# Earlier B copies, a split shared between DVE and ACT, and three drives moved from DVE to POOL in a Mamba scan

## What is computed

```python
x_d, z = jnp.split(jnp.einsum('btm,im->bti', x, W_in), 2, axis=-1)
x_d = _silu(conv_over_4_tokens(x_d) + conv_b)
dt_raw, B_mat, C_mat = split(jnp.einsum('btd,kd->btk', x_d, W_x))      # 1 + 16 + 16 columns
delta = jax.nn.softplus(dt_raw * W_dt[:, 0] + b_dt)
def step(h, inp):
    d_t, b_t, c_t, u_t = inp
    dA = jnp.exp(d_t[..., None] * A)
    h = dA * h + d_t[..., None] * b_t[:, None, :] * u_t[..., None]
    return h, jnp.einsum('bds,bs->bd', h, c_t)
y = (ys + D_param * x_d) * _silu(z)
h = _layernorm(x + y @ W_out.T)
scores = sigmoid(h @ gate_w.T)       # the best 4 of 8 groups, then 8 experts, weights normalised
out = _layernorm(h + experts(h) + shared(h))
```

## Time and profile before

| | |
|---|---|
| median of 3 runs | 1238.26 us (1237.28 to 1240.08) |
| the profiled execution's own time | 1239.62 us |
| its span, first to last instruction | 1237.8 us |
| mean granted TensorE clock | 0.926 |
| busy: PE, DVE, ACT, POOL | 1001.2, 1012.7, 639.0, 780.3 us |
| slot 0 of tile 5 to slot 0 of tile 6 | 403.33 to 478.32 us |

### The profile page before, as it was taken

One profiled execution on the slowest core, in us unless ns is written; L12 is line 12 of the kernel. 1 busy time (PEld: TensorE's weight loads), 2 busy tenths in 40 slices (PEclk: granted clock), 3 DMA queues, 4 the chain that ended last, 5 costly groups with the idle time before them and its releaser, 6 DMA issues.

```text
span 1237.8 us, 16888 instructions
## 1 busy us (share of the span) xinstructions
PE 1001.2 (81%) x4739; PEld 764.4 (62%) x4739; DVE 1012.7 (82%) x1914; ACT 639.0 (52%) x1662; POOL 780.3 (63%) x935
## 2 busy tenths in 40 slices
PE   3898878988788987879888786765299999999960
PEld 3776656666566665666656564443178888888850
DVE  7499999999999999999999999893334477777763
ACT  1575554646446464554645546431056666666640
POOL 7234376776767677687776777667600367677675
PEclk7999999999999999999999999878599999999985
DMA  4399401111021120101101010157355688988872
GB/s 171 121 328 325 130 22 37 42 34 42 26 60 33 34 63 13 58 26 44 53 26 48 3 51 25 34 196 298 95 152 172 204 252 261 277 266 265 268 220 80
DMA packets 104475, 150.28 MB, mean 121 GB/s; under 512 B 13983, under 2 KB 91231, under 8 KB 103999
## 3 DMA queue, kind: packets, MB, share of 16 engines
q1 hardware_dynamic: 87487, 107.39, 26.8%
q0 software_dynamic: 16896, 41.80, 11.8%
HBM read 72.32 MB, written 76.82 MB: 120 GB/s over the span
## 4 chain that ended last, share of the span: by engine, by line
DVE 39%; PE 29%; issue 15%; POOL 6%; DMA 1%; ACT 0%; DVEq 0%; SPq 0%; POOLq 0%; ACTq 0%
DVE arena L1320 20%; PE BC L979 11%; PE Y L826 4%; DVE arena L1307 3%; PE Y L973 3%; PE K L991 3%; PE F L991 3%; POOL gat L688 2%; DVE arena L1332 2%; PE K L838 2%; POOL pool_dram L627 2%; PE D L985 1%; DVE arena L1288 1%; DVE arena L1283 1%; DMA mixer_own<-pool_dram 1%
## 5 line engine op out<-in xcount | busy, mean ns | idle before, releaser
L1320 DVE TENSOR_TENSOR_SCAN arena<-D,arena 128x444 f32<-128x444 f32 (+1 forms) x352 | 350.9, 1037 | 6.3 <-ACT D L1067 5.2
L826 PE MATMUL Y<-arena,ident 128*128 128x444 f32 (+1 forms) x704 | 311.0, 571 | 1.6 <-DVE arena L1332 1.6
L688 POOL DMA_INDIRECT gat<-y_dram,slot_all x176 | 174.9, 994 | 148.6 <-DMA y_dram<-mixer_own 84.8
L1067 ACT ACTIVATE D<-mixer_own,aneg 128x216 f32<-128x216 f32 (+1 forms) x384 | 150.5, 427 | 151.5 <-DVE arena L1320 148.5
L1067 ACT ACTIVATE D<-arena,aneg 128x216 f32<-128x216 f32 x320 | 128.8, 438 | 141.2 <-DVE arena L1320 141.1
L627 POOL DMA_INDIRECT pool_dram<-hrow,slot_of x176 | 169.1, 961 | 49.4 <-issue 42.6
L639 POOL TENSOR_TENSOR arena<-mixer_own,arena 128x888 f32<-128x888 f32 (+1 forms) x72 | 130.8, 1816 | 101.2 <-ACT arena L1055 99.8
L1332 DVE TENSOR_TENSOR arena<-arena,BC 128x888 f32<-128x888 f32 (+1 forms) x176 | 184.7, 1049 | 4.6
L979 PE MATMUL BC<-arena,xt 128*128 x716 | 185.4, 382 | 0.1
L826 PEld LDWEIGHTS Y<-arena,ident 128*128 128x128 f32 x704 | 128.9, 202 | 76.0 <-issue 71.4
L639 POOL TENSOR_TENSOR arena<-arena 128x888 f32<-128x888 f32 x60 | 114.9, 1914 | 92.0 <-ACT arena L1055 89.7
(11 more groups left out here) (233 smaller groups left out, 1695.2 us busy)
## 6 DMA issues: line engine op xcount, KB each, us to landing
mixer_own<-pool_dram SPq DMA_DIRECT2D x179, 144.0 KB, 3.8
y_dram<-mixer_own SPq DMA_DIRECT2D x179, 128.0 KB, 3.1
pool_dram<-filler SPq DMA_DIRECT2D x5, 4176.0 KB, 31.4
arena<-in_experts_dram SPq DMA_DIRECT2D x1, 7680.0 KB, 22.7
arena<-in_x_dram SPq DMA_DIRECT2D x10, 648.0 KB, 4.0
pool_dram<-filler SPq DMA_DIRECT2D x1, 4896.0 KB, 34.5
arena<-in_experts_dram SPq DMA_DIRECT2D x1, 4608.0 KB, 14.7
pool_dram<-hrow,slot_of POOLq DMA_INDIRECT x176, 2.6
```

The lines of the kernel that those rows point to most:

```text
L688: nc.gpsimd.indirect_dma_start(out=gat[0:r, k, b, :], out_offset=None, in_=y_rows[0:blocks_by(t) * P, :], in_offset=bass.IndirectOffsetOnA ...
L826: mm = nc.tensor.matmul(Y[j][:, 0:w], ident[:], read[g % 3][:, j * w:(j + 1) * w], start=(s == 0), stop=(s == STATES - 1), skip_group_chec ...
L1067: last = nc.scalar.activation(D[b][:, c * w:(c + 1) * w].rearrange("p (a t) -> p a t", t=TOKENS)[:, :, 1:TOKENS], cut(delta[i % 2], i)[:, ...
L1320: nc.vector.tensor_tensor_scan(state[g % 2][:, lo:hi], D[b][:, 0:hi - lo], drive[g % DRIVES][:, lo:hi], 0.0, ALU.mult, ALU.add).then_inc(s ...
```

## The change

Four things, in tiles 0 to 10 where the pieces exist. The drives of states 6, 7 and 8 go from DVE to POOL (`OWN`), with three more `copy_b` on ACT. Scatters: slot 4's two go away and slots 10 and 11 have two each in place of one. In the slots of `B_FIRST` ACT does `copy_b(g + 2)` ahead of `decays(g + 1, 0)`; slot 14 in that list has no copy, since state 0 is DVE's. The roundings of `split` go to ACT (part 0 at the end of slot 10, part 1 in slot 11 between `softplus_exp` and the table load), DVE keeps two subtractions (slots 11 and 12), and DVE's copy of the middle part becomes a second rounding on ACT. The 1 that is added to the router's exponential goes from DVE to ACT. `tokens` goes ahead of `softplus_large`.

```diff
--- before.py
+++ after.py
@@ -50,8 +50,9 @@
 EARLY_EXPERTS = 20
 XG, YS, TOT = 8, 6, 3
 DRIVES, B_ROWS = 4, 4
-OWN = (0, 6, 7, 8)
-SCATTERS = (0, 0, 2, 2, 2, 0, 2, 2, 2, 2, 1, 1, 0, 0, 0, 0)
+OWN = (0,)
+B_FIRST = (1, 8, 9, 10, 11, 12, 13, 14)
+SCATTERS = (0, 0, 2, 2, 0, 0, 2, 2, 2, 2, 2, 2, 0, 0, 0, 0)
 MAGIC = float(2 ** 23)
 
 AHEAD = XG - 3
@@ -322,6 +323,7 @@
         h1t_done = sem("h1t_done")
         h1t_copied = sem("h1t_copied")
         logits_done = sem("logits_done")
+        ex_taken = sem("ex_taken")
         ex_done = sem("ex_done")
         route_step = sem("route_step")
         route_gate = sem("route_gate")
@@ -1034,6 +1036,19 @@
                 if c == KI - 1:
                     last.then_inc(dt_taken, 1)
 
+            def split(n, part):
+
+                w, at, rows = width(n), SPLITS * n, bc_rows[n % 2]
+                if part == 0:
+                    act.wait_ge(rows_done, n + 1)
+                    if n > 1:
+                        act.wait_ge(bc_done, STATES * (n - 1) + 1)
+                    nc.scalar.activation(rows[:, 0:w], K[0:SPLIT, N:N + w], ACT.Copy).then_inc(bc_split, 1)
+                    return
+                act.wait_ge(bc_split, at + 2)
+                nc.scalar.activation(mid[:, 0:w], rest[:, 0:w], ACT.Copy)
+                nc.scalar.activation(rows[ROWS:2 * ROWS, 0:w], rest[ROWS:2 * ROWS, 0:w], ACT.Copy).then_inc(bc_split, 1)
+
             def softplus_exp(n):
                 act.wait_ge(dt_taken, n + 1)
                 nc.scalar.activation(cut(soft, n), cut(soft, n), ACT.Exp, scale=-1.0).then_inc(soft_exp, 1)
@@ -1096,7 +1111,9 @@
                 if t > 0:
                     act.wait_ge(weights_done, t)
                 nc.scalar.activation(ex[0:h], K[0:h, LOGITS:LOGITS + 2 * EXPERTS].rearrange("p (b e) -> p b e", b=2), ACT.Exp,
-                                     scale=-1.0).then_inc(ex_done, 1)
+                                     scale=-1.0).then_inc(ex_taken, 1)
+                act.wait_ge(ex_taken, t + 1)
+                nc.scalar.activation(ex[0:h], ex[0:h], ACT.Identity, bias=one_col[0:h]).then_inc(ex_done, 1)
 
             def shared_gate(t):
                 act.wait_ge(shared_gu, t + 1)
@@ -1134,8 +1151,11 @@
                         take_dt(n, c)
                 if back and mix and s == 10:
                     take_ranks(t)
+                if front and s == 10:
+                    split(n, 0)
                 if front and s == 11:
                     softplus_exp(n)
+                    split(n, 1)
                     nc.scalar.preload_act_table_set("natural_log_exp_and_others")
                     softplus_ln(n)
                 if mix and s in (12, 14):
@@ -1146,10 +1166,13 @@
             for i in range(-1, TILES + 1):
                 for s in range(STATES):
                     g = STATES * i + s
+                    pooled_next = 0 <= g + 2 < STATES * TILES and by_pool(g + 2)
+                    if pooled_next and s in B_FIRST:
+                        copy_b(g + 2)
                     for b in range(2):
                         if 0 <= g + 1 < STATES * TILES:
                             decays(g + 1, b)
-                        if b == 0 and 0 <= g + 2 < STATES * TILES and by_pool(g + 2):
+                        if b == 0 and pooled_next and s not in B_FIRST:
                             copy_b(g + 2)
                     pieces(i, s)
 
@@ -1262,19 +1285,15 @@
                 nc.vector.scalar_tensor_tensor(cut(x2[n % 2], n)[:, 2 * b:2 * b + 2, :], cut(half_tanh, n)[:, 2 * b:2 * b + 2, :], 1.0,
                                                pair(F, n), ALU.add, ALU.mult).then_inc(x2_done, 1)
 
-            def split(n):
+            def split(n, part):
+
                 w, at = width(n), SPLITS * n
                 rows, bank = bc_rows[n % 2], K[:, N:2 * N]
-                dve.wait_ge(rows_done, n + 1)
-                if n > 1:
-                    dve.wait_ge(rank_taken, n - 1)
-                nc.vector.tensor_copy(rows[:, 0:w], bank[0:SPLIT, 0:w]).then_inc(bc_split, 1)
-                dve.wait_ge(bc_split, at + 1)
-                nc.vector.tensor_tensor(rest[:, 0:w], bank[0:SPLIT, 0:w], rows[:, 0:w], ALU.subtract).then_inc(bc_split, 1)
-                dve.wait_ge(bc_split, at + 2)
-                nc.vector.tensor_copy(mid[:, 0:w], rest[:, 0:w]).then_inc(bc_split, 1)
+                if part == 0:
+                    dve.wait_ge(bc_split, at + 1)
+                    nc.vector.tensor_tensor(rest[:, 0:w], bank[0:SPLIT, 0:w], rows[:, 0:w], ALU.subtract).then_inc(bc_split, 1)
+                    return
                 dve.wait_ge(bc_split, at + 3)
-                nc.vector.tensor_copy(rows[ROWS:2 * ROWS, 0:w], mid[ROWS:2 * ROWS, 0:w])
                 nc.vector.tensor_tensor(rows[2 * ROWS:SPLIT, 0:w], rest[2 * ROWS:SPLIT, 0:w], mid[2 * ROWS:SPLIT, 0:w],
                                         ALU.subtract).then_inc(bc_split, 1)
 
@@ -1394,7 +1413,6 @@
                 dve.wait_ge(ex_done, t + 1)
                 if t > 0:
                     dve.wait_ge(slots_done, t)
-                in_turn(nc.vector.tensor_scalar(ex[0:h], ex[0:h], 1.0, None, ALU.add))
                 in_turn(nc.vector.reciprocal(score[0:h], ex[0:h]))
                 in_turn(nc.vector.tensor_reduce(gsum[0:h, :, 0:GROUPS], score[0:h].rearrange("p b (g e) -> p b g e", g=GROUPS), AX.X, ALU.add))
                 for b in range(2):
@@ -1517,16 +1535,16 @@
                     shared_expert(t)
                 if back and mix and s == 9:
                     residual(t)
-                if front and s == 11:
-                    split(n)
+                if front and s in (11, 12):
+                    split(n, s - 11)
                 if front and s == 12:
                     softplus_small(n)
                 if mix and s in (13, 15):
                     silu_z(i, (s - 13) // 2)
+                if i + 2 < TILES and s == 13:
+                    tokens(i + 2)
                 if front and s == 13:
                     softplus_large(n)
-                if i + 2 < TILES and s == 13:
-                    tokens(i + 2)
                 if front and s == 14:
                     softplus_sum(n)
                     delta_x(n)
```

## The result

The changed kernel takes 1216.88 us (median of 4, 1215.85 to 1220.01), the kernel before 1238.89 (median of 4, 1237.28 to 1240.08): ratio 0.9824, 95% interval 0.9804 to 0.9843, 22 us less. The prediction was 1213 with 1194 to 1231.

A forecast was written before the change was run, and what follows sets the result against it. DVE sets the period, with PE, ACT and POOL each binding in places. Tiles 2 to 9 gain 8 x 2.4 = 19.2, tile 1 4, the last tile 3, tiles -1 and 0 -1: together 25, 1213 us, range 1194 to 1231.

The forecast's parts named there:

- three idle places named: DVE idle 3 to 4 us per tile: ahead of `shared_expert`, of state 13's scan and of `softplus_sum`.
- Slots 1 to 8, PE: PE works 25 us without a wait, so only 1.0 of the 2.5 us that DVE's drives free is gained.
- Slots 8 to 10: DVE: 1.3 earlier at slot 9 despite the router meeting drive 10 (0.4 to 1.1), 2.8 earlier at slot 11.
- Slots 10 to 12, ACT: ACT has no gap; three roundings add 1.0 us (0.7 to 1.3), and drive 13 starts at 449.9, not 452.14.
- Slots 11 to 14, POOL: POOL is full from drive 13 to the multiply's end, 16.0 us with the second scatter; gain 2.4 us per tile.
- rival A: POOL is not the end; DVE sets the time again from slot 11: 4.6 us per tile, 1195, chance 0.15.
- Tile 1: No scatters on POOL there, so only ACT's chain binds: a gain of 4 us.
- Tiles -1 and 0: Roundings lie on ACT's path, about 1.0 lost each, against some drives gained: -1 us.
- The last tile: POOL binds up to its first scatter behind the tiles, at 849.87: a gain of 3 us.
- B (the lock turns on POOL): POOL waits behind DVE's softplus pieces, 1.6 less gain per tile: 1226, chance 0.16; sign: POOL's 128x888 instructions exceed 1.9 and 2.9.
- C (decays behind the copy): Slots 8 to 13: decays wait behind B's copy for late spreads, so scans wait: slower, 1260, chance 0.08.
- D: ACT's and POOL's additions eat the gain, drive 13 not before 452: within 0.2% of before, chance 0.05.

The follow-up runs named there:

- scat_7_15: The changed kernel with one of slot 7's scatters in slot 10 and one of slot 11's in slot 15: 1322.88 us, 0.9744 of the kernel before.
- split_scat: The changed kernel with the whole split on DVE in slot 11 and the scatters placed as in `scat_7_15`: 1322.50 us, 0.9707 of the kernel before.
- scat_15: The changed kernel with one of slot 11's two scatters in slot 15: 1330.93 us, 0.9796 of the kernel before.
- after_again: The changed kernel run once more, unaltered, on another chip: 1337.65 us, 0.9835 of the kernel before.
- split_back: The changed kernel with the whole split on DVE in slot 11 again: 1211.25 us, 0.9773 of the kernel before.

## Why the prediction was right, point by point

**Time and mechanism.** 1216.88 against 1213. The time, the gain per tile and most of the places are as predicted, but two of the places were met with luck: two errors that cancel. The period is 72.50 against a predicted 72.6, and `wsel`, `masked` and `softplus_small` came to 0.22, 0.22 and 0.62. Of the three idle places named, two were found, not the one ahead of `shared_expert`. Tile 5 from its gate (403.33 before, 394.05 after; predicted places from the prediction's clock times or gains):

| place | before | predicted | after, tile 5 | tile 6 | mean of 2 to 9 |
|---|---|---|---|---|---|
| `act_s` | 31.12 | 30.1 | 29.28 | 28.62 | 28.7 |
| scan 9 | 35.19 | 33.9 | 34.57 | | 33.8 |
| scan 11 | 46.47 | 43.7 | 44.54 | | 43.8 |
| drive 13 | 48.81 | 46.6 | 47.24 | 46.58 | 46.6 |
| multiply's end | 63.60 | 62.6 | 63.17 | 62.55 | 62.6 |
| `softplus_sum` | 65.29 | 62.9 | 63.33 | 62.66 | 62.7 |

Tile 5 is one of the long ones (73.0): `slot_all` met drive 3 there and took 1.89, against 0.16 in tile 6. In the mean every place but `act_s` is met to some 0.2.

**Slots 1 to 8, PE: the size was off, by PE's clock.** DVE gained 1.8 in tile 5 and 2.5 in tile 6, nearly all that the drives free, not 1.0, and waited for `tanh_s` once in ten tiles (0.9 us). I had taken PE's 25 us from the spread to the shared expert as fixed. They weren't. In tile 5 before, PE waited 2.70 us for DVE, then its granted clock was 0.50 (the lower level), and its eight `Y` matmuls took 4.86 us; after, it waited 0.27, the clock was 1.00 (2.4 GHz), and the same eight took 3.16. The two rows, and then a stretch inside each (length; PE, PEld, DVE, ACT, POOL; clock; DMA), each time before and after:

```profile
407.80 4.86 PE L826 MATMUL Y<-arena,ident 128*128 128x444 f32 x8
```

```profile
398.52 3.16 PE L828 MATMUL Y<-arena,ident 128*128 128x444 f32 x8
```

```profile
409.00:412.00 3.00, 3.00 (x5) 1.35 (x4) 2.96 (x4) 1.78 (x5) 1.16 (x1) 0.50 0.00 0
```

```profile
399.00:402.00 3.00, 3.00 (x11) 1.63 (x10) 3.00 (x3) 1.84 (x6) 1.44 (x1) 1.00 0.00 0
```

Of tiles 2 to 9, seven had the 4.86 before and none has it after, and `tanh_s` comes 1.0 earlier in the mean. Why the low stretch moved no run was made to show. In the tiles 2 to 9 where it is back (six of `scat_7_15`, three of `split_scat`, one each of `scat_15` and `after_again`), so is a wait of 1.45 for `tanh_s`.

**Slots 8 to 10: the collision was right, its price 2 to 5 times too low.** I took 0.4 to 1.1 us for the router's last steps beside drive 10. The `glist` copy takes 2.3 us in most tiles (median 2.34, 0.17 before). I had counted the drive alone and not the scatter ahead of it, with which the wait begins. In the mean of tiles 2 to 9 slot 9's scan comes 1.3 earlier, the number predicted, and that is luck: 1.3 more was gained up to `act_s` than I said, and as much more lost behind it.

**Slots 10 to 12, ACT: right.** Taken 1.0 for the three roundings, bounds 0.7 and 1.3. Their rows show 0.37, 0.42 and 0.39 busy, and from the first one's start to the next instruction's 0.23 for the first (it overlaps), 0.43 and 0.41: 1.07.

```profile
440.60 0.37 ACT L1046 ACTIVATE bc_rows<-K 96x222 bf16<-96x222 f32 x1
...
443.36 0.42 ACT L1049 ACTIVATE mid<-rest 96x222 bf16<-96x222 f32 x1
443.79 0.39 ACT L1050 ACTIVATE bc_rows<-rest 32x222 bf16<-32x222 f32 x1
```

DVE's wait behind them is free, as I had it: in `split_back` it goes and the multiply still comes later than DVE. But `split_back` shows that the place of the first rounding, ahead of drive 13's copy, isn't: 0.2 per tile of the 5.6 us that it gains. I had counted it there as part of the chain, and hadn't asked whether the split was better left on DVE.

**Slots 11 to 14, POOL: right as the bound, its length with luck.** From drive 13 to the end of the multiply 15.93 us in tile 5 (441.29 to 457.22), predicted 16.0, and `softplus_sum` starts 0.16 behind. But I had added one scatter to a chain that I took as otherwise unchanged, and its parts changed. The multiply, which before had waited for `softplus_large`, got 0.84 shorter, as this row of before shows:

```profile
464.06 2.91 POOL L645 TENSOR_TENSOR arena<-arena 128x888 f32<-128x888 f32 x1
```

The first of four `prefix` steps, which had waited for `softplus_small`, got 0.37 shorter. In turn `seen` (0.70 from 0.27) now waits for `softplus_small` and `new_off` (0.94 from 0.25) for `softplus_large`: 1.12 longer. `scat_15` confirms the bound by taking its wait away, and shows how little lies behind it: `softplus_large` then meets drive 15, and 0.5 us per tile are all that is won. So rival A (1195) would have needed more than a freer POOL; with both joints eased the period was 70.9, not 70.4.

**Tile 1: the mis-sized term.** Predicted 4, from ACT's chain alone; measured 0.5 in the profiled execution and 2.8 in `after_again`. POOL has no scatters there, but its drives still meet DVE: `gmask` 1.73 in the one execution and 0.17 in the other, `chosen` 1.13 and `softplus_large` 2.63 in both.

**The sum.** Tiles -1 and 0: -0.7 (predicted -1). Tile 1: 0.5 (4). Tiles 2 to 9: 19.6 (19.2). The last tile to the first scatter behind it, 849.87 to 828.28 with all before it taken off: 2.2 (3). Together 21.6 instead of 25. The profiled execution gives 2.3 of it back in the experts' stage, where nothing was changed; the medians, 22.0 apart, don't.

**Rivals.** B (the lock turns on POOL) does happen: `seen` and `new_off`, issued inside `softplus_small` and `softplus_large`, wait for them, 1.12 us per tile in tile 5, of the 1.6 that B had. It isn't a loss against before, because 1.21 of such waits, in the multiply and in `prefix`, went. Its sign was looked for in the wrong place: POOL's 128x888 instructions stay at 1.9 and the multiply at 2.07. C (decays behind the copy) isn't there as a loss: in tile 5 ACT's long wait for a spread lies in slot 1 (4.40 us), and in slots 9 to 13 there is one of 0.73. D is ruled out by the interval.

**The Trainium skill's rule.** The Trainium skill (Perfetto Trace Analysis, Optimizing Scalar/DVE Operations) warns that moving work between VectorE and GpSimd "might not help". Here it did help, by 1.2% with the drives alone; the 2.2 us that the `glist` copy then waits per tile in the changed kernel are what the warning is about.

## What to carry to other kernels

When work moves from DVE to POOL, lay out not only its length but what is queued on POOL ahead of it: a small DVE copy or tensor_scalar issued in a scatter waited here for the scatter and for the drive right behind it. Place such pieces behind a drive that a scatter follows, or move the scatter; rewriting the stalled instruction alone handed the wait to the next one. Before you take an engine's length in a slot as fixed, look at what stretched it in the trace of before: here a low granted clock on PE and waits for DVE on POOL, and both changed with the edit. In a loop with three engines near their limits, test each part of a change by undoing it: here one part (the roundings on ACT) lost time, and undoing it, with two scatters moved, gained another 15.2 us, 1.1%.

## What the runs showed of the hardware that I had not expected

- An 8-column copy took up to 2.51 us, 15 times its 0.17, from one scatter (0.94) and one drive (1.91). In the 0.02 to 0.03 us between the two DVE didn't get in; behind the drive the next scatter stands 0.15 to 0.17 us off, and there it did. Between drive 15 and the multiply, queued with no gap, a DVE piece issued during the drive got in too: it took 2.65, and the multiply 2.91 instead of 2.07.
- Eight 128x444 matmuls took 4.86 us behind a wait of 2.70, at a granted clock of 0.50 for most of them, and 3.16 at 1.00. The stretch of low clock moved from tile to tile and from kernel to kernel.
- A tensor_reduce of the same tiles at the same place took 0.16 us in all ten tiles.
- The same program took 1216.88 us on one chip and 1337.65 on another, and nearly all of the difference lies behind the last scatter: 345 us in the changed kernel's profile and 464 in `after_again`'s, while up to the last scatter the two agree to 2 us. Its cause wasn't looked for.
